# Moving the second half's query loads to another place in the DMA order, and reordering the first three turns of a fused decoder layer

## The chip, the cores and the metric

The kernel runs on one core of a Trainium2 chip. The metric is the device time of one execution in microseconds, the median over several runs.

## The reference

One decoder layer on x (8 batches, 100 tokens, 512 features) with a context of 722 rows per batch. The change touches the middle part, the cross attention:

```python
x = x + rg_lru(layernorm(x))                       # gates, a scan over the tokens, an output product
ln = layernorm(layernorm(x), gamma_lat, beta_lat)  # latents, the queries' source
xn = layernorm(ctx, gamma_media, beta_media)       # 722 rows per batch
q = ln @ Wq + bq
k, v = split(concatenate([xn, ln]) @ Wkv + bkv)
out = softmax(q * DH**-0.5 @ k.T) @ v              # 8 heads of 128
x = x + out @ Wo + bo
x = x + moe(layernorm(x))                          # 8 experts, one chosen per token, gelu
```

## The kernel before, in words

The key weights are folded into the queries, so that scores are products of a query row of 512 numbers per head with the normed context itself, and the value weights are applied after the weighted sum over the context. Every float32 product is made of three float32r products: both operands are split into a high part (a copy on ScalarE, `..._h`) and a low part (the difference, on VectorE, `..._l`); `split_products` (L585, L586, L587) issues the three matmuls.

The attention runs in 16 **turns** u = 2b + g: batch b, half g of the heads (4 heads, 100 tokens, 400 columns). The context's 722 rows and the 100 latents make 7 row tiles (KC = 7). Turn u on TensorE is: `scores(u, 0..6)` (six tiles of 12 matmuls, one of 8), with `spread_sums(u-1)` (L1162, small matmuls that sum the weights of the turn before over the partitions) behind tile 3; then the four quarters of `context(u-1)` (20 matmuls each; L585 to L587, L1186, L1187), with `turn_maxima(u)` (transposes, L1149) behind the first quarter and `spread_maxima(u)` (L1156) behind the second. Turn 0 has scores alone.

VectorE in turn u: `weights(u-1)` (sums and low parts of the exponentials, L1961 to L1972; its last sum releases `spread_sums`), `first_maximum` (L1918), `inverse(u-1)` (L1992, waits for `spread_sums`), `last_maximum` (L1924 to L1932, releases `turn_maxima`), `shifts` (L1941 to L1947, writes dg, which `spread_maxima` waits for), `shift` (L1955, the maxima are added to the scores), and `weighted` (L2001, evacuates a quarter of the context). Between these stand the preparations of later turns: `queries(b, g)` (L1735 qt_l<-qf,qt_h), `keys_transposed` (L1893), `keys_centred` (L1882, needs the row means), `rows_stats` (L1719), `rows_norm` (L1731), `rows_low` (L1908). ScalarE has the matching high parts: `queries` (L1446), `evacuate` (L1475), `exponentials` (L1484), `weights_high` (L1490), `rows_high`, `add_shift` (L1498).

Nothing schedules this: each engine has its order written out by hand, and semaphores join them. SyncE issues nearly all DMAs, in one order of its own, and stands at each wait: for batch b of its loop the latents' keys, the raw context rows of b + 2, the half of the queries (b+1, 1), the transposed context `rt` of b + 2, the store of the sum z(b, 0), the queries (b+2, 0), the store of z(b, 1), a bias row. The queries (800 KB per half batch) go through **one** buffer, `qf`; a load waits until VectorE has made the low part of what was there (`s_qtl`). GpSimd issues the small DMAs: `store_mean` writes the row means to DRAM (L919), `load_mean` brings them back as a row on all partitions (L925), and `spread_inverse` does the same with the inverse sums (L930, L932, L935).

```python
                sp.wait_ge(s_qtl, 2 * (b + 1) + 1)
                load_queries(b + 1, 1)
                sp.wait_ge(s_ktl, keys_done(b + 1))
                if b + 2 < B:
                    load_keys(b + 2)
                write_z(b, 0)
```

After turn 15 comes the `tail` list: value products "V", high and low parts of the units "U", splits of the output weights "O", and so on, interpreted on each engine by its own `finish`. The buffers of the value weights share their place with those of the attention: `rt`, `mrow` and `raw1` lie over `wv_h`.

Of the kernel before, what the change touches and what calls it, by code (L numbers as in the profile page):

```python
# [133 lines left out]
def build(nc, a, out):  # L134
# [59 lines left out]
    raws = [raw, mem.over(wv_h, "raw1", [P, KC, D], skip=ND * MEDIA + -(-MEDIA // 16) * 16)]  # L194
    assert ND * MEDIA + -(-MEDIA // 16) * 16 + KC * D <= 2 * ND * INNER
# [263 lines left out]
    tail = [("V", 0), ("C", 0), ("U", 4), ("V", 1), ("O", 0), ("U", 5), ("V", 2), ("O", 1), ("U", 6), ("V", 3), ("O", 2),  # L459
# [130 lines left out]
    with ctx:  # L590
# [3 lines left out]
        def _(sp):  # L594
# [184 lines left out]
            for b in range(B - 1):  # L779
# [23 lines left out]
            sp.wait_ge(s_xnl, 3 * B)  # L803
            sp.dma_start(wv[:], a["Wv"].rearrange("(c p) n -> p c n", p=P)).then_inc(s_wvd, 16)
# [38 lines left out]
        def _(pool):  # L843
# [146 lines left out]
        def _(pe):  # L990
# [271 lines left out]
            for u in range(1, NU):  # L1262
                for c in range(KC):
# [5 lines left out]
                    elif u > 1 and c == 3:  # L1269
# [92 lines left out]
        def _(act):  # L1362
# [137 lines left out]
            def values_high(k):  # L1500
                act.wait_ge(s_wvd, 16)
                act.copy(wv_h[:, k, :], wv[:, k, :]).then_inc(s_wvh, 1)

            def output_high(k):
                if k == 0:
                    act.wait_ge(s_wod, 16)
# [99 lines left out]
            for u in range(1, NU):  # L1606
# [15 lines left out]
                else:  # L1622
                    weights_high(u - 1, 0)
                    evacuate(u, 0)
                    add_shift(u - 2, ND - 1)
# [9 lines left out]
                    else:  # L1635
                        evacuate(u, 2)
                        queries(b, 1)
                        evacuate(u, 3)
                    for c in range(4, KC):
                        evacuate(u, c)  # L1640
                if g and b + 1 < B:
                    for k in range(ND):
                        keys_transposed(b + 1, k)
                elif not g and b + 1 < B:
                    queries(b + 1, 0)
                add_shift(u - 1, 0)
                if u < NU - 1:
# [4 lines left out]
                    exponentials(u, 2)  # L1652
            for part in range(NP):
# [718 lines left out]
```

## Time and profile before

| | us |
|---|---|
| median of 3 runs | 1032.45 |
| the runs | 1032.45, 1033.51, 1027.98 |
| the profiled execution's own time | 1042.73 |
| its span | 1041.0 |
| TensorE busy | 999.5 (96%) |
| VectorE busy | 821.5 (79%) |
| ScalarE busy | 585.0 (56%) |
| mean granted TensorE clock | 0.985 |

The span is what the trace covers, from the first to the last instruction; the 1.7 us around it belong to the execution's own time. Busy shares are means over very unlike stages. In the rows below a time in brackets is the idle time of that engine just before the row, and behind the arrow stands what ended it.

### The profile page before, as it was taken

Reading aid. Unit: us, or ns where it says so; the run is one execution under the profiler, and the core shown is the slowest. Engines: PE = TensorE matmul, PEld = TensorE weight load, DVE = VectorE, ACT = ScalarE, POOL = GpSimd, SP = SyncE. Lnnn points to the kernel's source line nnn. Section 1 sums busy time; section 2 is a strip of 40 time slices with the busy share of each in tenths; the row PEclk is TensorE's granted clock in tenths of the full one; section 3 lists DMA queues with packets and bytes.
Section 4 is the critical chain, followed back from the end, with each engine's and each line's share of the span. In section 5 each row is a group of like instructions: output and inputs, shape, how many; then the busy total and the mean of one; then the engine's idle time right before and its main releaser. Section 6 shows DMA issues by size and latency. Waiting matters only on the chain.

```text
span 1041.0 us, 14901 instructions
## 1 busy us (share of the span) xinstructions
PE 999.5 (96%) x5274; PEld 919.8 (88%) x5275; DVE 821.5 (79%) x1083; ACT 585.0 (56%) x766; POOL 167.7 (16%) x169
## 2 busy tenths in 40 slices
PE   8999999989999999998999999999999999999995
PEld 6969999879999999998999999998867888888884
DVE  7888456898999989897898977885768947938981
ACT  4426565545546565464554646673645846838861
POOL 3715000111111111111111000000111211211220
PEclk9999999989999999999899999999998999999998
DMA  9433879462654818356184212978358956938960
GB/s 266 135 114 122 302 252 290 122 129 73 177 92 116 161 54 193 75 158 119 55 191 77 88 40 95 312 265 291 120 156 295 356 196 214 347 136 281 362 229 8
DMA packets 107117, 183.88 MB, mean 177 GB/s; under 512 B 27936, under 2 KB 48928, under 8 KB 107058
## 3 DMA queue, kind: packets, MB, share of 16 engines
q1 hardware_dynamic: 102834, 172.64, 54.7%
q0 software_dynamic: 4224, 10.46, 4.2%
q8 instruction: 37, 0.61, 0.2%
q14 instruction: 22, 0.18, 0.1%
HBM read 146.94 MB, written 37.11 MB: 177 GB/s over the span
## 4 chain that ended last, share of the span: by engine, by line
PE 66%; DVE 15%; DMA 9%; issue 4%; ACT 2%; SPq 2%; POOL 0%; DVEq 0%; ACTq 0%; POOLq 0%
PE bank L585 19%; PE bank L586 18%; PE bank L587 18%; DMA qf<-scr_q 6%; DVE str__65 L1719 2%; PE bank L1337 2%; DMA w<-in_WoT 1%; PE bank L1061 1%; DVE pa L1955 1%; DVE xt_l L1893 1%; PE bank L1063 1%; PE bank L1062 1%; DMA zr<-scr_z 1%; DVE hs L1808 1%; PE bank L1156 1%
## 5 line engine op out<-in xcount | busy, mean ns | idle before, releaser
L1735 DVE TENSOR_TENSOR wsl<-stage,wsh 128x2048 fp32r<-128x2048 f32 x63 | 143.7, 2291 | 23.6 <-ACT wsh L1525 18.6
L585 PE MATMUL bank<-ph,xn_h 128*128 128x400 f32 x384 | 140.2, 365 | 0.0
L585 PE MATMUL bank<-qt_h,xt_h 128*128 128x400 f32 x384 | 134.3, 350 | 0.0
L586 PE MATMUL bank<-pl,xn_h 128*128 128x400 f32 x384 | 133.4, 347 | 0.0
L586 PE MATMUL bank<-qt_l,xt_h 128*128 128x400 f32 x384 | 132.7, 346 | 0.0
L587 PE MATMUL bank<-ph,xn_l 128*128 128x400 f32 x384 | 132.7, 345 | 0.0
L587 PE MATMUL bank<-qt_h,xt_l 128*128 128x400 f32 x384 | 132.1, 344 | 0.0
L1525 ACT CAST wsh<-stage 128x2048 fp32r<-128x2048 f32 x63 | 120.5, 1919 | 11.0 <-PE bank L587 8.0
L1475 ACT ACTIVATE pa<-bank,rsr 128x400 f32<-128x400 f32 x96 | 56.4, 591 | 76.0 <-PE bank L587 75.9
L1498 ACT ACTIVATE zf<-zf,gbm 128x400 f32<-128x400 f32 x64 | 39.5, 627 | 105.0 <-DVE zf L2001 105.0
L585 PEld LDWEIGHTS bank<-ph,xn_h 128*128 128x128 f32 x384 | 73.3, 191 | 2.5 <-DVE zf L2001 0.6
L586 PEld LDWEIGHTS bank<-pl,xn_h 128*128 128x128 f32 x384 | 73.3, 191 | 2.3 <-issue 0.3
L587 PEld LDWEIGHTS bank<-ph,xn_l 128*128 128x128 f32 x384 | 73.1, 190 | 0.0
L585 PEld LDWEIGHTS bank<-qt_h,xt_h 128*128 128x128 f32 x384 | 72.8, 190 | 0.2
L586 PEld LDWEIGHTS bank<-qt_l,xt_h 128*128 128x128 f32 x384 | 72.6, 189 | 0.2
L587 PEld LDWEIGHTS bank<-qt_h,xt_l 128*128 128x128 f32 x384 | 72.5, 189 | 0.0
L585 PE MATMUL bank<-wsh,xg_h 128*128 128x512 f32 x160 | 64.8, 405 | 2.4 <-issue 2.4
L585 PE MATMUL bank<-wsh,ht_h 128*128 128x512 f32 x160 | 65.1, 407 | 0.0
L587 PE MATMUL bank<-wsh,xg_l 128*128 128x512 f32 x160 | 63.5, 397 | 0.0
L586 PE MATMUL bank<-wsl,xg_h 128*128 128x512 f32 x160 | 63.4, 397 | 0.0
L587 PE MATMUL bank<-wsh,ht_l 128*128 128x512 f32 x160 | 62.6, 391 | 0.0
L586 PE MATMUL bank<-wsl,ht_h 128*128 128x512 f32 x160 | 62.3, 390 | 0.0
(278 smaller groups left out, 2368.7 us busy)
## 6 DMA issues: line engine op xcount, KB each, us to landing
stage<-in_W SPq DMA_DIRECT2D x63, 1024.0 KB, 6.3
scr_q<-st SPq DMA_DIRECT2D x16, 800.0 KB, 6.7
qf<-scr_q SPq DMA_DIRECT2D x16, 800.0 KB, 7.5
scr_z<-zf SPq DMA_DIRECT2D x16, 800.0 KB, 4.5
zr<-scr_z SPq DMA_DIRECT2D x16, 800.0 KB, 6.2
rt<-in_ctxT SPq DMA_DIRECT2D x7, 1444.0 KB, 21.9
raw<-in_ctx SPq DMA_DIRECT2D x8, 768.0 KB, 5.7
raw<-in_ctx SPq DMA_DIRECT2D x8, 512.0 KB
```

Source lines behind the costliest of these rows:

```text
L585: pe.matmul(dest, lh, rh, start=start and k == 0, stop=False)
L586: pe.matmul(dest, lh, rl, start=False, stop=False)
L587: last = pe.matmul(dest, ll, rh, start=False, stop=stop and k == n - 1)
L1061: pe.matmul(wide, high, xa_h[:, c, tokens_and_shift], start=c == 0, stop=False)
L1062: pe.matmul(out_tokens, high, xa_l[:, c, cols], start=False, stop=False)
L1063: last = pe.matmul(wide, low, xa_h[:, c, tokens_and_shift], start=False, stop=c == ND - 1)
L1337: last = pe.transpose(bank[2 + k % 2][:, c * P:(c + 1) * P], hid[k % 2][:, c * P:(c + 1) * P], ident[:])
L1475: act.activation(pa[k][:, c, :], score_bank(u, c)[:, 0:GR], ACT.Identity, scale=rss[b % 2][:, c:c + 1]).then_inc(s_ev, 1)
L1498: act.activation(at, at, ACT.Identity, bias=gbm[:, 1, dc:dc + 1]).then_inc(s_zbeta, 1)
L1525: act.copy(wsh[q][:], (first_last if made_in_place else stage[q % 4])[:]).then_inc(s_wh, 1)
L1719: ch.add(dve.bn_stats(str_[0:r, c, :], r0[0:r, c, :]))
L1735: return dve.tensor_tensor(dst, src, high.bitcast(F32), ALU.subtract)
```

## The change

Six edits, on all engines.

- **Loads.** SyncE requests the queries (b+1, 1) no longer before `rt` of b + 2 (only for b = 0), but those of (b+2, 1) between the stores of z(b, 0) and z(b, 1); the queries (b+2, 0) go ahead of the store of z(b, 0).
- **Splits of queries.** ScalarE and VectorE make `queries(b+1, 1)` at the end of the odd turn 2b+1, in place of `queries(b, 1)` in the even turn 2b.
- **Turns 1 and 2.** VectorE makes `shifts(1)` ahead of `queries(1, 0)` and the four `keys_transposed`, all four `weighted(0, ...)` behind `shift(1)`, and moves `rows_stats(2)`, `rows_norm(1)` and `queries` in turn 2.
- **Sums.** TensorE makes `spread_sums(1)` behind score tile 6 of turn 2 instead of tile 3.
- **Means.** GpSimd stores the means of batch 2 behind `spread_inverse(1)`, no longer ahead of it.
- **Value weights.** `rt` and `mrow` lie over `wv`, `raw1` over `wv_h`; `wv` is loaded in SyncE's loop, `values_high` and two of four `values_low` go into turn 15, and the first split of the output weights ahead of the last `weighted`.

```diff
+    wv = mem("wv", [P, ND, INNER])
     wv_h = mem("wv_h", [P, ND, INNER], F32R)
-    wv = mem("wv", [P, ND, INNER])
...
-    rt = mem.over(wv_h, "rt", [P, ND, MEDIA])
-    mrow = mem.over(wv_h, "mrow", [P, MEDIA], skip=ND * MEDIA)
+    rt = mem.over(wv, "rt", [P, ND, MEDIA])
+    mrow = mem.over(wv, "mrow", [P, MEDIA], skip=ND * MEDIA)
+    raws = [raw, mem.over(wv_h, "raw1", [P, KC, D], skip=ND * INNER - KC * D)]
...
-    tail = [("V", 0), ("C", 0), ("U", 4), ("V", 1), ("O", 0), ("U", 5), ("V", 2), ("O", 1), ("U", 6), ("V", 3), ("O", 2),
+    tail = [("V", 0), ("C", 0), ("U", 4), ("V", 1), ("O", 1), ("U", 5), ("V", 2), ("O", 2), ("U", 6), ("V", 3),
...
-                sp.wait_ge(s_qtl, 2 * (b + 1) + 1)
-                load_queries(b + 1, 1)
+                if b == 0:
+                    sp.wait_ge(s_qtl, 3)
+                    load_queries(1, 1)
                 sp.wait_ge(s_ktl, keys_done(b + 1))
                 if b + 2 < B:
                     load_keys(b + 2)
+                    sp.wait_ge(s_qtl, 2 * (b + 1) + 2)
+                    load_queries(b + 2, 0)
+                else:
+                    sp.dma_start(wv[:], a["Wv"].rearrange("(c p) n -> p c n", p=P)).then_inc(s_wvd, 16)
                 write_z(b, 0)
                 if b + 2 < B:
-                    sp.wait_ge(s_qtl, 2 * (b + 1) + 2)
-                    load_queries(b + 2, 0)
+                    sp.wait_ge(s_qtl, 2 * (b + 2) + 1)
+                    load_queries(b + 2, 1)
                 write_z(b, 1)
...
-                if b + 2 < B:
+                if 0 < b < B - 2:
                     store_mean(b + 2)
                 spread_inverse(2 * b + 1)
+                if b == 0:
+                    store_mean(2)
...
-                    elif u > 1 and c == 3:
+                    elif u > 1 and c == (KC - 1 if u == 2 else 3):
                         spread_sums(u - 1)
...
+                    shifts(1)
                     queries(1, 0)
+                    for k in range(ND):
+                        keys_transposed(1, k)
+                    for part in range(NP):
+                        shift(1, part)
+                    for dc in range(ND):
+                        weighted(0, dc)
+                    continue
+                if u == 2:
+                    weights(1)
+                    first_maximum(2)
+                    inverse(1)
+                    rows_stats(2, 0)
+                    last_maximum(2)
+                    rows_stats(2, 1)
+                    shifts(2)
+                    weighted(1, 0)
+                    queries(1, 1)
+                    weighted(1, 1)
+                    for part in range(NP):
+                        shift(2, part)
+                    weighted(1, 2)
+                    rows_norm(1, 0)
+                    rows_norm(1, 1)
+                    keys_centred(2, 0)
+                    keys_centred(2, 1)
+                    queries(2, 0)
+                    continue
...
-                if g and b + 2 < B:
-                    rows_stats(b + 2, 0)
-                    rows_stats(b + 2, 1)
-                elif not g and b + 1 < B:
+                if g:
+                    if b + 2 < B:
+                        rows_stats(b + 2, 0)
+                        rows_stats(b + 2, 1)
+                    queries(b + 1, 1)
+                elif b + 1 < B:
                     keys_centred(b + 1, 0)
                     keys_centred(b + 1, 1)
             u = NU - 1
             shifts(u)
+            values_low(0)
             weighted(u - 1, 0)
             for part in range(NP):
                 shift(u, part)
             weighted(u - 1, 1)
+            values_low(1)
             first_sum(u)
...
-            for k in range(ND):
+            for k in range(2, ND):
                 values_low(k)
             low_unit(0)
             low_unit(1)
+            output_low(0)
```

What the diff shows less well is what now stands in a row. First VectorE, in turn 1, between the means taken off the keys of batch 1 and the last exponentials' sums (dg is what `spread_maxima(1)` waits for). Before:

```order
L1882 TENSOR_TENSOR rt<-rt,mrow 128x1444 x2
L1735 TENSOR_TENSOR qt_l<-qf,qt_h 128x4x400
L1893 SCALAR_TENSOR_TENSOR xt_l<-rt,gbm,xt_h 128x722 x3
L1941 TENSOR_REDUCE rm<-bank 100x4
L1943 TENSOR_TENSOR rmc<-rm,c_0_106 100x4
L1945 TENSOR_TENSOR nb<-c_0_106,rmc 100x4
L1947 TENSOR_TENSOR dg<-ident,nb 100x400
```

Now:

```order
L1904 TENSOR_TENSOR rt<-rt,mrow 128x1444 x2
L1963 TENSOR_REDUCE rm<-bank 100x4
L1965 TENSOR_TENSOR rmc<-rm,c_0_106 100x4
L1967 TENSOR_TENSOR nb<-c_0_106,rmc 100x4
L1969 TENSOR_TENSOR dg<-ident,nb 100x400
L1757 TENSOR_TENSOR qt_l<-qf,qt_h 128x4x400
L1915 SCALAR_TENSOR_TENSOR xt_l<-rt,gbm,xt_h 128x722 x4
L1977 TENSOR_TENSOR pa_93<-pa_93,bank 128x1200 x2
```

The four instructions that lead to dg moved ahead of one split of queries and four of keys.

Second VectorE, at the border of every later odd turn and the even turn behind it (here turns 7 and 8), from the last row statistics to the first maximum of the even turn. Before:

```order
L1724 BN_AGGR mvr_104<-str__65 82x2
L2001 TENSOR_TENSOR zf_82<-bank,inv 128x4x100
L1961 TENSOR_TENSOR sm<-pa_93 128x800
L1735 TENSOR_TENSOR pl_96<-pa_93,ph_94 128x1200
L1965 TENSOR_TENSOR sm<-sm,pa_93 128x800
L1735 TENSOR_TENSOR pl_96<-pa_93,ph_94 128x1200
L1969 TENSOR_TENSOR sm<-sm 128x400
L1972 TENSOR_TENSOR sm<-sm,pa_93 54x400
L1735 TENSOR_TENSOR pl_96<-pa_93,ph_94 54x400
L1735 TENSOR_TENSOR qt_l<-qf,qt_h 128x4x400
L1918 TENSOR_TENSOR mx<-pa_91 128x800
```

Now:

```order
L1746 BN_AGGR mvr_104<-str__65 82x2
L1757 TENSOR_TENSOR qt_l<-qf,qt_h 128x4x400
L2023 TENSOR_TENSOR zf_82<-bank,inv 128x4x100
L1983 TENSOR_TENSOR sm<-pa_93 128x800
L1757 TENSOR_TENSOR pl_96<-pa_93,ph_94 128x1200
L1987 TENSOR_TENSOR sm<-sm,pa_93 128x800
L1757 TENSOR_TENSOR pl_96<-pa_93,ph_94 128x1200
L1991 TENSOR_TENSOR sm<-sm 128x400
L1994 TENSOR_TENSOR sm<-sm,pa_93 54x400
L1757 TENSOR_TENSOR pl_96<-pa_93,ph_94 54x400
L1940 TENSOR_TENSOR mx<-pa_91 128x800
```

One split of queries moved from behind the sums (L1972, now L1994) to ahead of them.

Third VectorE, the end of turn 2 as it stands now, from the last quarter but one of the context to the first sum of turn 3 (`raw_80` is the buffer of batch 1's rows, `mrow` the means of batch 2):

```order
L2023 TENSOR_TENSOR zf_99<-bank,inv 128x4x100
L1753 SCALAR_TENSOR_TENSOR raw_80<-raw_80,mvr_104,gm 128x512 x5
L1753 SCALAR_TENSOR_TENSOR raw_80<-raw_80,mvr_104,gm 82x512
L1904 TENSOR_TENSOR rt<-rt,mrow 128x1444 x2
L1757 TENSOR_TENSOR qt_l<-qf,qt_h 128x4x400
L2023 TENSOR_TENSOR zf_99<-bank,inv 128x4x100
L1983 TENSOR_TENSOR sm<-pa_91 128x800
```

The norms of batch 1's rows and a split of queries, which stood ahead of dg in turn 2, now stand around the keys' centring and ahead of the sums of turn 3.

## Rows read from the trace of the kernel before

**Rows 1.** The page: busy time of each engine.

```profile
PE 999.5 (96%) x5274; PEld 919.8 (88%) x5275; DVE 821.5 (79%) x1083; ACT 585.0 (56%) x766; POOL 167.7 (16%) x169
```

**Rows 2.** Waits on PE, 300 to 640 us: total, times, longest, in us.

```profile
PE bank L1149 <- DVEq L1712: 6.4, 2, 5.2
PE bank L1156 <- DVE dg L1947: 1.8, 3, 0.7
```

**Rows 3.** Timeline of PE: start us, us, line, operation, count, [idle before <-releaser].

```profile
210.84 1.65 PE L1156 MATMUL bank<-dg,ones 100*128 100x400 f32 x2 [4.25 <-DVE dg L1947]
...
227.55 1.13 PE L1162 MATMUL bank<-ones,sm 128*100 128x1 f32 x8 [1.73 <-DVEq L1712]
...
235.59 0.35 PE L1141 MATMUL bank<-qt_l,xt_h 128*128 128x400 f32 x1
...
239.22 0.35 PE L1187 MATMUL bank<-pl,xn_h 128*128 128x400 f32 x1
...
260.15 0.43 PE L1162 MATMUL bank<-ones,sm 128*100 128x1 f32 x4
...
416.76 0.61 PE L1162 MATMUL bank<-ones,sm 128*100 128x1 f32 x6
...
699.95 0.45 PE L585 MATMUL bank<-z_h,wv_h 128*128 128x400 f32 x1 [1.48 <-DVE z_l L1735]
```

**Rows 4.** Busy time, granted clock and DMA share of single stretches.

```profile
core 0: us, PE busy (x) PEld busy (x) DVE busy (x) ACT busy (x) POOL busy (x), PEclk, DMA share, GB/s
208.00:216.00 8.00, 5.17 (x18) 4.49 (x19) 7.90 (x12) 2.46 (x3) 0.88 (x1) 0.79 0.60 197
228.00:232.00 4.00, 4.00 (x17) 3.97 (x17) 4.00 (x6) 0.00 (x0) 0.58 (x1) 0.57 0.75 53
492.00:504.00 12.00, 8.28 (x32) 7.94 (x33) 8.81 (x14) 2.78 (x3) 4.50 (x5) 0.72 0.19 50
696.00:704.00 8.00, 6.53 (x32) 5.90 (x33) 8.00 (x9) 7.69 (x10) 0.00 (x0) 1.00 0.89 309
391.80:416.40 24.60, 24.60 (x137) 24.25 (x137) 23.54 (x37) 13.68 (x19) 2.85 (x4) 1.00 0.89 204
```

**Rows 5.** Timeline of DVE, turns 1 and 2, and the last sum of turn 7.

```profile
200.91 3.23 DVE L1882 TENSOR_TENSOR rt<-rt,mrow 128x1444 f32<-128x1444 f32 x2 [0.21 <-DVE mx L1932]
204.06 1.82 DVE L1735 TENSOR_TENSOR qt_l<-qf,qt_h 128x1600 fp32r<-128x1600 f32 x1
205.80 2.73 DVE L1893 SCALAR_TENSOR_TENSOR xt_l<-rt,gbm,xt_h 128x722 fp32r<-128x722 f32 x3
...
208.44 0.68 DVE L1941 TENSOR_REDUCE rm<-bank 100x4 f32<-100x512 f32 x1
...
212.55 3.18 DVE L1955 TENSOR_TENSOR pa<-pa,bank 128x1200 f32<-128x1200 f32 x3
...
221.58 0.98 DVE L1961 TENSOR_TENSOR sm<-pa 128x800 f32<-128x800 f32 x1
...
230.80 4.03 DVE L1731 SCALAR_TENSOR_TENSOR raw<-raw,mvr,gm 128x512 f32<-128x512 f32 x6
...
235.13 0.99 DVE L1924 TENSOR_TENSOR mx<-mx,pa 128x800 f32<-128x800 f32 x1 [0.30 <-ACT pa L1475]
...
415.77 0.57 DVE L1972 TENSOR_TENSOR sm<-sm,pa 54x400 f32<-54x400 f32 x1
```

**Rows 6.** Timeline of POOL: an inverse sum on its way through DRAM.

```profile
263.74 0.67 POOL L930 DMA_DIRECT2D scr_inverse<-iv  x1 [19.89 <-DVE iv L1992]
...
269.75 0.98 POOL L935 COPY inv<-sm 128x400 f32<-128x400 f32 x1 [3.35 <-DMA sm<-scr_inverse]
```

**Rows 7.** DMAs that touch mvr (stores of the means).

```profile
DMA to landing us min/median/max: 8.5/10.4/12.8
```

**Rows 8.** DMAs that touch mrow (loads of the means).

```profile
DMA to landing us min/median/max: 3.5/3.7/5.5
```

**Rows 9.** The chain, 455 to 490 us: start us, us, what.

```profile
461.00 23.67 DMA qf<-scr_q
```

**Rows 10.** DMAs that touch qf (loads of queries).

```profile
DMA to landing us min/median/max: 4.8/7.5/23.7
```

More of the change, by code:

```diff
@@ L1624, in _ @@
                     evacuate(u, 0)
-                    add_shift(u - 2, ND - 1)
+                    if u > 2:
+                        add_shift(u - 2, ND - 1)
                     weights_high(u - 1, 1)
@@ L1636, in _ @@
                         evacuate(u, 2)
-                        queries(b, 1)
                         evacuate(u, 3)
+                        if u == 2:
+                            for dc in range(ND):
+                                add_shift(0, dc)
                     for c in range(4, KC):
@@ L1643, in _ @@
                         keys_transposed(b + 1, k)
+                elif u == 2:
+                    queries(1, 1)
                 elif not g and b + 1 < B:
                     queries(b + 1, 0)
+                elif u == NU - 1:
+                    for k in range(ND):
+                        values_high(k)
+                if u == 1:
+                    for part in range(NP):
+                        exponentials(1, part)
+                    continue
                 add_shift(u - 1, 0)
@@ L2130, in _ @@
                         keys_centred(1, half)
+                    shifts(1)
                     queries(1, 0)
-                else:
-                    weighted(u - 2, ND - 1)
-                    weights(u - 1)
-                    if g:
-                        rows_low(b, 0)
-                        first_maximum(u)
-                        inverse(u - 1)
-                        rows_low(b, 1)
-                        rows_low(b, 2)
-                        last_maximum(u)
-                    else:
-                        queries(b, 1)
-                        first_maximum(u)
-                        inverse(u - 1)
-                        rows_norm(b, 0)
-                        rows_norm(b, 1)
-                        last_maximum(u)
+                    for k in range(ND):
+                        keys_transposed(1, k)
+                    for part in range(NP):
+                        shift(1, part)
+                    for dc in range(ND):
+                        weighted(0, dc)
+                    continue
+                if u == 2:
+                    weights(1)
[6 more added lines that the diff above has]
+                    weighted(1, 0)
+                    queries(1, 1)
+                    weighted(1, 1)
+                    for part in range(NP):
+                        shift(2, part)
[4 more added lines that the diff above has]
+                    keys_centred(2, 1)
+                    queries(2, 0)
+                    continue
+                weighted(u - 2, ND - 1)
+                weights(u - 1)
+                if g:
+                    rows_low(b, 0)
+                    first_maximum(u)
+                    inverse(u - 1)
+                    rows_low(b, 1)
+                    rows_low(b, 2)
+                    last_maximum(u)
+                else:
+                    first_maximum(u)
+                    inverse(u - 1)
+                    rows_norm(b, 0)
+                    rows_norm(b, 1)
+                    last_maximum(u)
                 if u == NU - 1:
@@ L2186, in _ @@
             inverse(u)
-            for k in range(ND):
+            for k in range(2, ND):
                 values_low(k)
```

16 lines of the change are left out of this document (9 added, 7 removed).

## The prediction

> **What bounds the kernel now.** First the page: TensorE is busy 999.5 of 1041.0 us, VectorE 821.5 [rows 1]. So a change that adds no matmul can win only TensorE's idle time, 41 us over the whole program, and the time that its matmuls take too long after its clock has fallen. Second, who makes TensorE wait, in its list of waits and its timeline. In turns 1 and 2 it waits 4.25 us for dg (`shifts(1)`) and 1.73 us for the sums of turn 1 [rows 3]. From 300 to 640 us it waits five times, 8.2 us together, of which one is 5.2 us (turn 9, at the maxima) and four others, with 0.7 the longest of their three at dg, make 3.0 us [rows 2]. Third, the clock in the windows around them: behind the 4.25 us it is 0.79 over 8 us, a loss of 0.21 x 8 = 1.7 us; behind the 1.73 us 0.57 over 4 us, again 1.7 us; around the 5.2 us 0.72 over 12 us, 3.4 us at most, and I take 2.6 us since part of it fell into the wait. These are stretches at the lower of the two levels, 1.2 instead of 2.4 GHz. Behind a wait of 1.48 us at 700 us it stayed at 1.00 [rows 3, 4]. Fourth, what lies behind the 5.2 us: the chain shows a load of queries of 23.67 us, against a median of 7.5 [rows 9, 10]; VectorE stood behind it, in front of the even turn's maxima.
>
> Fifth, VectorE itself. In turns 1 and 2 it has almost no idle time: it is VectorE, not TensorE, that sets the pace there. And in the later odd turns it is just as tight: from 391.8 to 416.4 us it is busy 23.54 of 24.6 us, the rest being the small spaces between dependent instructions [rows 4]; its last sum of turn 7 ends at 415.77 + 0.57 = 416.34 and TensorE needs it at 416.76 [rows 3, 5]. That is a margin of 0.42 us, 0.3 after the 0.1 that a released instruction takes.
>
> **Turns 1 and 2: +2.9 us.** Durations are distances between starts in rows 5: centring 3.15, a split of queries 1.74, a split of keys 0.88, the four instructions to dg 2.3 (208.44 to the 210.78 just before TensorE's release), `shift` 3.1, a `weighted` 0.5, the sums 5.9 (to 227.44) and 0.6 for the last low part, the norms 4.0, `last_maximum` 2.7, a `first_maximum` 0.9. The two `rows_stats` take 2.5 each (what lies between `shift` and the sums less one `weighted`). A matmul takes 3.63/20 = 0.18 [rows 3].
>
> Now VectorE goes: centring to 204.05, dg at 206.4, queries 208.1, four keys 211.6, `shift` 214.7, four `weighted` 216.7, weights 223.2, first maximum 224.1. TensorE, free for dg at 206.6, no longer waits 4.25 us; it makes one quarter of context and starts the scores of turn 2 at 211.7, when the keys are there. But `spread_sums(1)` now stands behind all 80 matmuls of them: 211.7 + 14.5 = 226.2, done at 226.8. VectorE has to wait for it in `inverse(1)`, 2.7 us, where it waited for nothing before. Then statistics 229.3, last maximum 232.0: TensorE, through a quarter at 230.5, waits 1.5 us for it. Statistics, dg at 236.8, then one `weighted`, queries, `weighted`, `shift`, `weighted`, norms: 247.1.
>
> There stands the centring of batch 2's keys, and it needs the row of means. GpSimd now stores the means behind `spread_inverse(1)`: released at 226.9, 7.0 us for the way of the inverse through DRAM (263.74 to 270.73) [rows 6], so 233.9; the second of two stores starts 0.9 us later and lands after 10.4 (8.5 to 12.8) [rows 7], at 245.2; the load takes 3.7 (3.5 to 5.5) [rows 8]: 249.0. VectorE waits 1.9 us. Then 3.15 + 1.74 + 0.5 + 5.9 = 11.3: the sum of turn 2 at 260.3, and TensorE can make its `spread_sums(2)` at 260.4, where it made it at 260.15 [rows 3]. Its own work would have brought it there at about 253.6 (dg at 236.8, 0.8 for its two small matmuls, two quarters 7.3, four score tiles of 12 matmuls 8.7), so it waits some 7 us in one piece, longer than the 5.2 us, and the clock falls behind it: 2.6 us as there. Together 0.3 + 2.6 = +2.9. The gain of 4.25 and 1.73 us at TensorE is not there to be had, because VectorE's same work, with two new waits, decides.
> Bounds: with the means in time and a clock loss of 1.7 only, -0.1; if dg's four instructions also take 0.7 less each time, -1.5. With 12.8 and 5.5 for store and load, the wait is 6.1 us and the clock costs 3.4: +8.3.
>
> Here the Trainium skill says something else (DMA: Bandwidth & Descriptors, "Anatomy of one DMA", the gpsimd path): a DMA takes about 2.0 us and its bytes over 436 GB/s, by which a store of 1.5 KB would be an estimated 2.0 us and the means never late. The rows have 8.5 to 12.8 [rows 7], so the trace does not agree, and the sum goes by the rows.
>
> **Turns 4 to 14: +7.2 us, and -4.2 us.** The split of queries (b+1, 1), 1.74 us, moves from behind the last sum to ahead of the chain that leads to it, and nothing leaves that chain: from the evacuations that TensorE releases to the sum it holds the same instructions as before. So at each `spread_sums` of an odd turn TensorE will wait 1.74 - 0.3 = 1.43 us. Turns 6, 8, 10 and 12 have this margin (0.41 or 0.42), turn 4 even less; turn 14 has 1.6 and is left out. 5 x 1.43 = 7.2. Bounds: 5.0 (if half of the small spaces close up) and 8.7 (1.74 each).
> In exchange the four small waits of the even turns go, -3.0 [rows 2], and an ordinary one of 1.2 in the place of the long one, together -4.2: they come from the split of queries and the late landing ahead of the maxima; now one split stands there, loaded earlier, and TensorE is later by 1.4. For the long one see below. Nothing else in the even turn changes: the queries (b+2, 0) are requested some 7 us earlier, and those of (b+2, 1) a whole turn before use, so a landing of 23.67 us [rows 9] is hidden there. Behind SyncE's new wait stands the store of z(b, 1) alone, whose data come half a turn later anyway; z(b, 0) is needed only a turn on.
>
> **Value weights and tail: -0.5 us.** `values_low(1)` stands ahead of the first sum of turn 15 and delays it by some 0.8 us; a split of the output weights leaves the tail's chain ahead of the wait of 1.48 us [rows 3] and shortens it by up to 1.2. Bounds -1.5 and +0.8. The weights' load, 2 MB, moves to a stretch with little other traffic: nothing.
>
> **The sum.** Against the profiled execution: 1042.73 + 2.9 + 7.2 - 3.0 - 7.8 (5.2 and 2.6 of clock) - 0.5 = 1041.5. That execution is 10.3 us above the median of the runs, and the long wait of 7.8 us explains most of it, so I take it that the median run does not have it, only an ordinary wait of 1.2 us in its place. Against the median then: 1032.45 + 2.9 + 7.2 - 4.2 - 0.5 = **1037.9 us**. With the bounds of the terms it is 1031 to 1045.
>
> **The rivals.**
> - *The long wait was in the median run too.* For it: one load of sixteen took 23.67 and the runs spread over 5.5 us. Against it: the 10.3 us. Then 1032.45 + 2.9 + 7.2 - 3.0 - 7.8 - 0.5 = 1031.3.
> - *Faster: VectorE has room.* The waits at the sums and the early stall do not appear, because what I read as a full VectorE gives way once queries never hold it, and the loads' waits were everywhere: 1032.45 - 3.0 - 7.8 - 0.5 = 1021.2; with half of the new waits 1026. For it: VectorE is busy only 79% overall [rows 1]. Against: rows 4 and the margin of 0.42.
> - *Slower: waits of 1.4 us bring the clock down.* It fell behind 1.73 us but not behind 1.48 [rows 3, 4]. If it falls five times for 1.7 us: 1037.9 + 8.5 = 1046.4. It decides as soon as the waits reach the 1.7 us of turn 2.
> - *The first half's queries become the late ones, so the change only moves the wait.* They are now requested behind `rt` and beside the stores of the means, and needed 0.5 + 6.5 + 1.0 + 4.0 + 2.7 = 14.7 us later, less 1.5 for the high part. 7.5 us [rows 10] is in time; 23.67 each time would cost (23.7 - 13.2 - 2 of margin) + 2.6 per batch, 11 us, and even two such batches give 1060. The Trainium skill speaks for this rival (same page, "Issuing engines are not separate DMA queues"): DMAs of all engines interleave on the same 16 engines. What the row shows is that a load of queries beside such traffic took three times the median.
> - *The means come as that page prices them.* No wait at the centring, sum of turn 2 at 258.5 instead of 260.3: 1037.9 - 1.8 = 1036.1. The landings speak against it [rows 7].
>
> **How the numbers follow.** The forecast has 0.43, half of it above 1037.6 and half within 0.5% (a measurement of this kernel can tell about 0.5%, 5 us, from no change); the long wait in the median 0.15 (same); room on VectorE 0.20 (faster); the clock 0.10 (slower); late first halves 0.06 (slower); means in time 0.06 (same). Faster 0.20, same 0.42, slower 0.38. The range from 1026 to 1046 leaves out most of the rival with room and the worst of the slow ones.
>
> **What would show it.** TensorE's wait for dg in turn 1 is gone; a new one of some 7 us before `spread_sums(2)`, followed by a granted clock near 0.7; VectorE waits for GpSimd's DMA ahead of the centring of batch 2 (about 2 us) and for TensorE in `inverse(1)` (about 3 us). `spread_sums` of turns 5, 7, 9, 11 waits 1.4 us each at a clock of 1.00; the maxima and dg of even turns wait for nothing, and no load of queries appears in the chain. If TensorE waits at the sums of odd turns less than 0.5 us, or reaches the end of turn 2 before 255 us, the prediction is wrong.

## The result, and the profile after

| | before | after |
|---|---|---|
| median, us | 1031.14 | 1049.49 |
| runs, us | 1027.98 to 1033.51 (4) | 1048.25 to 1052.54 (4) |
| ratio, 95% interval | | 1.0184 [1.0147, 1.0222] |
| profiled execution, us | 1042.73 | 1049.27 |
| span, us | 1041.0 | 1047.5 |
| mean granted clock | 0.985 | 0.978 |

The change makes the kernel 1.8% slower: 18.35 us between the medians. The forecast of 1037.9 us had added 5.4 us to the median it started from (1032.45), and 1049.49 lies above its range. Later, in the series of the experiments, the changed kernel had a ratio of 1.014 [1.0071, 1.0210] to the kernel before beside it. The profiled execution of before is 11.6 us above its own median; a second profile of it (first experiment, "the good profile" from here on) has no such long wait, and is the better one to subtract.

Busy time of the engines, which answers to [rows 1]: 4.2 us more on TensorE for the same matmuls, at a mean granted clock of 0.978 in place of 0.985.

```profile
PE 1003.7 (96%) x5274; PEld 923.4 (88%) x5275; DVE 818.9 (78%) x1083; ACT 585.0 (56%) x766; POOL 171.8 (16%) x169
```

Waits on TensorE from 300 to 640 us (total, times, longest), the answer to [rows 2]. All waits at the maxima and at dg are gone; one kind is left, at the sums of the odd turns (turn 3's, at 298 us, lies just outside the stretch).

```profile
PE bank L1167 <- DVEq L1734: 5.0, 4, 1.3
```

TensorE's timeline (start, duration, line, operation, count, [idle time before and what ended it]), the answer to [rows 3]. L1154 are the maxima, L1167 the sums.

```profile
232.70 0.64 PE L1154 MATMUL bank<-ident,mx 128*100 128x128 f32 x4 [1.74 <-DVEq L1734]
...
263.19 1.49 PE L1167 MATMUL bank<-ones,sm 128*100 128x1 f32 x8 [9.19 <-DVEq L1734]
...
298.03 0.87 PE L1167 MATMUL bank<-ones,sm 128*100 128x1 f32 x8 [1.53 <-DVEq L1734]
...
361.55 0.87 PE L1167 MATMUL bank<-ones,sm 128*100 128x1 f32 x8 [1.25 <-DVEq L1734]
...
426.51 0.87 PE L1167 MATMUL bank<-ones,sm 128*100 128x1 f32 x8 [1.26 <-DVEq L1734]
...
706.58 0.45 PE L585 MATMUL bank<-z_h,wv_h 128*128 128x400 f32 x1 [0.35 <-DVE z_l L1757]
```

The waits of 4.25 and 1.73 us in turns 1 and 2 have gone. In their place stand 1.74 us at the maxima of turn 2 and 9.19 us at its sums. Turn 3 waits 1.53 us at its sums, turns 5, 7, 9 and 11 wait 1.25 to 1.27 each. The wait before the value product fell from 1.48 to 0.35 us.

Granted clock in single stretches (columns as in [rows 4]):

```profile
core 0: us, PE busy (x) PEld busy (x) DVE busy (x) ACT busy (x) POOL busy (x), PEclk, DMA share, GB/s
258.00:262.00 4.00, 0.00 (x0) 0.00 (x0) 3.93 (x5) 3.96 (x7) 0.00 (x0) 0.50 0.94 325
262.00:266.00 4.00, 2.81 (x12) 2.80 (x13) 3.82 (x7) 4.00 (x8) 0.00 (x0) 0.50 0.29 71
298.00:302.00 4.00, 3.97 (x26) 3.97 (x27) 3.93 (x7) 0.60 (x1) 0.58 (x1) 1.00 0.60 86
426.00:430.00 4.00, 3.49 (x18) 3.46 (x19) 3.85 (x8) 0.00 (x0) 0.58 (x1) 0.75 0.57 56
430.00:434.00 4.00, 4.00 (x20) 3.98 (x20) 2.06 (x4) 1.16 (x2) 0.00 (x0) 0.82 0.75 310
```

Behind the 9.19 us, at 263, TensorE is at the lower level (0.50); behind the 1.53 us at 298 it stays at 1.00; behind the 1.26 us at 426 it has lost (0.25 + 0.18) x 4 = 1.7 us. Behind the sums of turns 5, 9 and 11 the same 1.7 us are lost. Behind the 1.74 us at the maxima of turn 2 the clock stayed at 1.00.

VectorE and GpSimd in turn 2, the answers to [rows 5] and [rows 6]:

```profile
227.28 0.18 DVE L2014 RECIPROCAL iv<-bank 100x4 f32<-100x4 f32 x1 [3.37 <-PE bank L1167]
...
251.85 1.66 DVE L1904 TENSOR_TENSOR rt<-rt,mrow 128x1444 f32<-128x1444 f32 x1 [4.60 <-DMA mrow<-scr_rows]
```

```profile
234.09 0.78 POOL L922 DMA_DIRECT2D scr_rows<-mvr  x1
...
235.41 0.77 POOL L922 DMA_DIRECT2D scr_rows<-mvr  x1 [0.55 <-DVEq L1734]
...
244.84 0.55 POOL L928 DMA_DIRECT2D mrow<-scr_rows  x1 [8.66 <-DMA scr_rows<-mvr]
```

VectorE waits 3.37 us for the sums behind tile 6 and 4.60 us for the row of means. GpSimd stores the means only when the inverse has come back (234.09), both stores have landed at 244.8, and the load takes another 7.0 us until VectorE goes on.

### The profile page after: what moved, and what is told of

Read it like the earlier page. It is cut to its first block, busy times and chain, and to the rows that moved or that the text cites. A ratio compares the mean times of both kernels' runs of the same rounds, so it can differ in the third digit from the quotient of the medians.

```text
span 1047.5 us, 14907 instructions
## 1 busy us (share of the span) xinstructions
PE 1003.7 (96%) x5274; PEld 923.4 (88%) x5275; DVE 818.9 (78%) x1083; ACT 585.0 (56%) x766; POOL 171.8 (16%) x169
## 4 chain that ended last, share of the span: by engine, by line
PE 76%; DVE 12%; issue 5%; DMA 3%; ACT 2%; POOL 0%; SPq 0%; DVEq 0%; ACTq 0%; POOLq 0%
PE bank L585 21%; PE bank L586 20%; PE bank L587 20%; DVE str__65 L1741 2%; PE bank L1342 2%; DVE xt_l L1915 2%; DVE pa L1977 1%; PE bank L1167 1%; PE bank L1066 1%; PE bank L1068 1%; PE bank L1067 1%; DVE zf L2023 1%; DMA xin<-in_x 1%; PE bank L1146 1%; PE bank L1145 1%
## 5 line engine op out<-in xcount | busy, mean ns | idle before, releaser
L585 PE MATMUL bank<-qt_h,xt_h 128*128 128x400 f32 x384 | 137.0, 357 | 0.3 <-issue 0.3
L586 PE MATMUL bank<-qt_l,xt_h 128*128 128x400 f32 x384 | 135.3, 352 | 0.0
L587 PE MATMUL bank<-qt_h,xt_l 128*128 128x400 f32 x384 | 134.7, 351 | 0.0
L1532 ACT CAST wsh<-stage 128x2048 fp32r<-128x2048 f32 x63 | 120.5, 1919 | 14.5 <-DMA stage<-in_W 8.8
L586 PE MATMUL bank<-wsl,ht_h 128*128 128x512 f32 x160 | 62.3, 390 | 0.0
```

The source lines that it names most:

```text
L585: pe.matmul(dest, lh, rh, start=start and k == 0, stop=False)
L586: pe.matmul(dest, lh, rl, start=False, stop=False)
L587: last = pe.matmul(dest, ll, rh, start=False, stop=stop and k == n - 1)
L1532: act.copy(wsh[q][:], (first_last if made_in_place else stage[q % 4])[:]).then_inc(s_wh, 1)
```

## The experiments

They ran in four groups on four chips, each beside the kernel before on the same chip, where its median was 1036 to 1039 us: the first five rows of the table but "changed, again" on one; "tile 4, no means stored", both "splits back" and "first turns alone" on the next; the other two without the means' stores, "value weights alone" and "statistics first" on the third; "changed, again" and "means first" on the last. So the ratio to the kernel before is what can be compared across them, and its intervals are wide (0.3 to 0.7% to each side). Beside it stand marks, each from one profile: *first turns* is the distance between the starts of the inverses of turns 0 and 3 on VectorE, *a batch* a quarter of that between turns 3 and 11, *way* the time from the inverse of an odd turn (5, 7, 9, 11; it is made in the even turn behind) to the start of its copy on all partitions by GpSimd. The first profile of the changed kernel has 101.2, 64.6 and 10.3 to 10.9, so its two profiles differ by 1.7 us in the first turns and by 0.1 us in a batch.

| kernel | ratio [95%] | first turns | a batch | way |
|---|---|---|---|---|
| before, again | 1.0000 [0.9959, 1.0041] | 96.4 | 62.9 | 8.5 to 10.3 |
| changed, again | 1.0140 [1.0071, 1.0210] | 102.9 | 64.7 | 11.2 to 11.9 |
| sums behind tile 4 | 1.0172 [1.0113, 1.0232] | 102.2 | 65.5 | 12.3 to 13.3 |
| filled waits | 1.0148 [1.0087, 1.0209] | 103.3 | 65.0 | 13.0 to 13.8 |
| first turns old | 1.0109 [1.0049, 1.0169] | 99.8 | 65.0 | 11.8 to 12.3 |
| tile 4, no means stored | 0.9991 [0.9959, 1.0023] | 103.4 | 62.1 | 6.3 to 7.6 |
| changed, no means stored | 1.0122 [1.0071, 1.0173] | 103.2 | 65.0 | 6.1 to 6.4 |
| filled, no means stored | 1.0093 [1.0056, 1.0130] | 104.0 | 63.9 | 6.1 to 6.5 |
| splits back | 0.9974 [0.9943, 1.0005] | 100.7 | 62.2 | 9.5 to 10.4 |
| splits back, first turns old | 0.9935 [0.9894, 0.9976] | 96.8 | 62.7 | 9.8 to 11.0 |
| first turns alone | 1.0024 [0.9988, 1.0060] | 100.6 | 63.9 | 9.0 to 10.9 |
| value weights alone | 0.9989 [0.9951, 1.0028] | 96.7 | 64.7 | 8.0 to 10.5 |
| statistics first | 0.9993 [0.9964, 1.0022] | 102.2 | 62.3 | 9.0 to 11.0 |
| means first | 1.0007 [0.9973, 1.0041] | 103.0 | 62.3 | 9.4 to 10.8 |

### Both kernels once more

> The kernel before, once more, for a second profile of it. Theory 'the long wait is a disturbance': no load of queries near 23.67 us, no wait of 5.2 us in turn 9, and a span near 1030 us instead of 1041. Rival 'it belongs to the kernel': a wait of 4 to 6 us at the maxima of some even turn again, span 1035 to 1041. Time against the kernel before: ratio 1.000, and its interval says how fine the comparison is.

Span 1033.2 us, no wait of 5.2 us, the longest load of queries in the attention 19.7 us. But its ten runs went from 1034.8 to 1044.0, so neither theory holds in full: by their times, some executions have a long wait and some not. The waits on TensorE from 300 to 640 us in this good profile, 2.1 us in all:

```profile
PE bank L1149 <- DVEq L1712: 1.5, 2, 0.9
PE bank L1156 <- DVE dg L1947: 0.6, 1, 0.6
```

> The changed kernel once more, beside the kernel before, on the chip of the experiments: its first result came from another one. Expected ratio 1.013 to 1.020, four batches of 65.0 us, waits of 1.26 us at the sums of turns 5 to 11. If it is under 1.010, what is said of the splits' place is too large.

As expected, with two exceptions. The first of the four batches (65.3 us) had a further wait of 1.5 us for an evacuated quarter in turn 4, and the second took 63.4 us in place of 65.0. There the wait at the sums (1.25 us, at 364.31) was as long as elsewhere, and the clock stayed up:

```profile
core 0: us, PE busy (x) PEld busy (x) DVE busy (x) ACT busy (x) POOL busy (x), PEclk, DMA share, GB/s
364.00:368.00 4.00, 3.69 (x24) 3.69 (x25) 3.85 (x8) 0.48 (x1) 0.58 (x1) 1.00 0.68 50
```

### The sums of odd turns one tile later

```diff
-                    elif u > 1 and c == (KC - 1 if u == 2 else 3):
+                    elif u > 1 and c == (KC - 1 if u == 2 else 4 if 4 <= u < NU and u % 2 == 0 else 3):
```

> The changed kernel with the sums of odd turns 3 to 11 made behind score tile 4 instead of 3, that is one tile of 12 matmuls (2.2 us) later on TensorE; nothing else moves. Theory 'the waits at the odd sums and the clock behind them': five waits (1.53 and four of 1.26) and four falls of the clock (1.7 us each) go, 6.6 + 6.8 = 13.4 us, 1049.5 - 13.4 = about 1036 us. Rival 'waits alone, the clock falls for another reason': 1043 us. Rival 'VectorE sets the pace of the odd turns anyway': the wait comes back at the next place that needs VectorE, and the time stays within 2 us of 1049.5.

(The edit moves the sums of turn 13 as well.) The waits at the sums were gone, and nothing was won: 1.0172. TensorE (first row) now waited for the evacuated quarter, VectorE (second) for the inverse sums, and GpSimd's timeline shows why: 7.7 us from the inverse's store to the load that waits for it, 5.1 more to the copy.

```profile
446.26 0.45 PE L585 MATMUL bank<-ph,xn_h 128*128 128x400 f32 x1 [2.79 <-DVE zf L2023]
```

```profile
445.63 1.06 DVE L2023 TENSOR_TENSOR zf<-bank,inv 128x400 f32<-128x400 f32 x2 [3.97 <-POOL inv L938]
```

```profile
421.80 0.75 POOL L922 DMA_DIRECT2D scr_rows<-mvr  x1 [1.69 <-DVEq L1734]
...
431.85 0.58 POOL L933 DMA_DIRECT2D scr_inverse<-iv  x1 [9.30 <-DVE iv L2014]
...
439.52 0.58 POOL L935 DMA_DIRECT2D sm<-scr_inverse  x1 [7.08 <-DMA scr_inverse<-iv]
...
444.66 0.89 POOL L938 COPY inv<-sm 128x400 f32<-128x400 f32 x1 [4.56 <-DMA sm<-scr_inverse]
```

The third theory is the nearest, but what sets the pace is not VectorE's work: it idles 4 us. It is the way of the inverse through DRAM, which begins with the sums.

### The waits filled with matmuls

```diff
+                pe.wait_ge(s_dg, u + 1)
+                if u % 2 and 3 < u < NU - 1:
+                    keep_running(mbank, xn_h[:, 0, :], 6)
                 pe.wait_ge(s_sum, u + 1)
-                pe.wait_ge(s_dg, u + 1)
```

> The changed kernel with six matmuls whose result nobody reads (512 columns each, some 1.3 us) ahead of TensorE's wait for the sums of turns 5, 7, 9, 11 and 13: TensorE is no longer idle there, but nothing comes earlier. Theory 'half of what the waits cost is the clock behind them': the granted clock stays at 1.00 behind the sums, and the time falls by 4 x 1.7 = 6.8 us to about 1042.7 (turn 13 pays some 1.1 us of filler for nothing: about 1044). Rival 'the clock falls at those places whatever TensorE does in the wait': 1049.5 to 1051 and the windows behind the sums stay at 0.75 to 0.8.

The clock behind the sums stayed at 1.00, where the changed kernel has 0.75 and 0.82:

```profile
core 0: us, PE busy (x) PEld busy (x) DVE busy (x) ACT busy (x) POOL busy (x), PEclk, DMA share, GB/s
426.00:430.00 4.00, 4.00 (x23) 3.91 (x22) 3.96 (x4) 3.13 (x6) 0.00 (x0) 1.00 0.55 24
430.00:434.00 4.00, 4.00 (x26) 3.60 (x26) 3.82 (x8) 0.16 (x2) 0.59 (x1) 1.00 0.89 37
```

The same held at the three other filled waits, and at turn 3's, left unfilled, the clock fell behind 1.63 us. So the fall belongs to TensorE's idling. But the time did not follow (1.0148), for the reason of the run before: no longer slowed by the clock, TensorE now reached the third quarter too early, and waited 0.8 to 1.7 us there for the first to be evacuated.

### The inverse's way without the stores of the means

> The kernel with the sums behind tile 4, and besides, for the batches from 3 on, the row means are not stored (one row in place of 128; the row of batch 1's means is loaded instead, so the outputs are not the layer's). What it is for: with the sums behind tile 4 the waits at the sums went, but TensorE then waited 1.8 to 3.2 us once a batch for the first evacuated quarter, since VectorE waited 4 us for the inverse sums, whose way through DRAM took 13.1 us (store 7.6, load 5.0) in even turns. Theory 'that store lies behind the element-wise stores of the means on the DMA engines': without them the store takes about 2 us as in the last even turn, the way 6 to 8 us, no wait for the quarter, a batch takes 62.6 us as before instead of 64.7, and the time is about 4 x 2.1 to 5 x 2.1 = 8 to 10 us under that of the sums behind tile 4, or 5 to 7 us above the kernel before. Rival 'it is the loads of queries and keys': the way stays above 11 us and a batch at 64.7.

```diff
-                    pool.dma_start(d_row[b].rearrange("(c p) -> p c", p=P)[:, cs], mvs[b % 2][:, cs, 0],
+                    n = P if b < 3 else 1
+                    pool.dma_start(d_row[b].rearrange("(c p) -> p c", p=P)[0:n, cs], mvs[b % 2][0:n, cs, 0],
...
-                pool.dma_start(mrow[:], bc(d_row[b, 0:MEDIA], MEDIA)).then_inc(s_mrow, 16)
+                pool.dma_start(mrow[:], bc(d_row[b if b < 3 else 1, 0:MEDIA], MEDIA)).then_inc(s_mrow, 16)
```

(Against the changed kernel the sums also stand behind tile 4 here.) The way fell from about 13 to between 6.3 and 7.6 us, a batch from 65.5 to 62.1, the ratio from 1.0172 to 0.9991. Of 300 to 640 us only one wait of TensorE was left:

```profile
PE bank L1155 <- DVEq L1735: 0.3, 1, 0.3
```

The stores of the means are what makes the inverse late. They also stretch the loads of the first halves' queries, which are requested just behind them: 4.9 to 5.2 us without the stores, 12.1 to 12.8 with them, at the same place behind the keys.

> The changed kernel as it is, but for the batches from 3 on the row means are not stored (one row in place of 128; batch 1's row is loaded, so the outputs are not the layer's). Theory 'the stores of the means cost time only through the inverse's way, and in the changed kernel the waits at the sums come first': the way shortens to 6 to 8 us, but the waits of 1.26 us at the sums and the clock falls behind them stay, a batch takes 64.5 to 65 us, ratio to before about 1.015 to 1.018. Rival 'the traffic of the means slows the changed kernel by itself': ratio near 1.005.

The way 6.1 to 6.4, the waits at the sums as in the changed kernel (below, with turn 3's now inside the stretch), a batch 65.0. In the changed kernel the sums bind first, and the way second, close behind.

```profile
PE bank L1168 <- DVEq L1735: 6.6, 5, 1.5
```

> The changed kernel without the stores of the means from batch 3 on (as above) and with six matmuls of 512 columns that nobody reads ahead of the waits for the sums of turns 5 to 13: the sums come when they came, but TensorE is busy meanwhile. Without the means' stores the inverse is in time, so the waits for the first quarter do not come. Theory 'half of the cost is the clock': it stays at 1.00 behind the sums and a batch takes 1.7 us less than in the kernel without filler, 63.2 us; 4 x 1.7 = 6.8 us less in all, ratio about 1.010. Rival 'the clock costs nothing, something else is just as late': no difference to the kernel without filler beyond 1 us.

The last three batches took 63.4 to 63.5 us each in place of 65.0, and the span fell from 1051.9 to 1047.0; the first, with turn 3's unfilled wait and a fall behind it, took 65.1. So the clock alone is 1.5 to 1.6 us a batch. The intervals of the two ratios overlap, so this rests on the profiles, on the single batch of 63.4 us above, and on the first batch of the changed kernel's first profile, which took 63.5 us where the clock stayed up behind turn 3's wait.

### The splits put back

```diff
+                    queries(b, 1)
                     first_maximum(u)
                     inverse(u - 1)
...
-                    queries(b + 1, 1)
```

(ScalarE's high parts move in the same way, and SyncE asks for z(b, 0), (b+2, 0), (b+2, 1) in this order)

> The changed kernel with the splits of the second half's queries put back behind the sums of the even turn (VectorE and ScalarE); the load (b+2, 1) stays a turn early, directly behind the load (b+2, 0), the store of z(b, 0) goes ahead of both as before; first turns and tail as changed. Theory 'the split ahead of the odd turn's sums is what costs 2.35 us per batch': no waits at the odd sums, the way of the inverse no longer decides (the sums come 1.7 us earlier), a batch takes 62.6 us or less, and the time is 13 to 14 us below the changed kernel: about 4 us above the kernel before (early turns +5.1, tail -1.2). Rival 'the early load's traffic costs it': a batch stays at 64 us or more, 10 us or more above the kernel before.

0.9974, a batch 62.2 us. All that is left of TensorE's waits between 300 and 640 us:

```profile
PE bank L1161 <- DVE dg L1969: 0.4, 1, 0.4
```

The whole loss of the later turns went with this edit, that is with the place of one split of 1.8 us on VectorE, ScalarE's copy for it, and the order of z(b, 0) and (b+2, 0) on SyncE; these three were not tried one by one. The early load of (b+2, 1) is not its cause, since it stayed.

### The first turns

> The changed kernel with its first three turns put back as they were before (VectorE, ScalarE, the sums of turn 1 behind tile 3, the means of batch 2 stored ahead of the second inverse); the loads' new place and the splits at the end of odd turns stay from turn 3 on. Theory (trace marks): the early part costs 5.1 us, so about 1044.4. By the prediction's own price of 2.9: 1046.6. Rival 'early order is neutral, both stalls only swapped': 1049 to 1050.

1.0109 against 1.0140 for the changed kernel (measured on another of the chips). A batch is 65.0 as there; the first turns are 3.1 us shorter than in its second profile, 1.4 than in its first, nearer to the prediction's own price of 2.9 than to 5.1. They still hold a wait of 3.1 us for the inverse in turn 2.

> The kernel before with the reordering of the first three turns alone (VectorE, ScalarE, the sums of turn 1 behind tile 6, the means of batch 2 behind the second inverse). Theory: +5.1 us (wait of 9 us at the sums of turn 2 and its clock, against 4.25 and 1.73 and theirs), ratio 1.005. The prediction's price was +2.9, ratio 1.003. Rival 'it is neutral': 1.000.

1.0024, which the interval [0.9988, 1.0060] does not tell from no change; in the profile the first turns are 4.2 us longer than before, with this wait at the sums of turn 2:

```profile
262.71 1.50 PE L1164 MATMUL bank<-ones,sm 128*100 128x1 f32 x8 [8.44 <-DVEq L1727]
```

> The kernel with the splits put back (first turns as changed), with the first half of the row statistics of batch 2 ahead of the inverse of turn 1 on VectorE in turn 2, where it waits 3.4 us for TensorE's sums. Theory 'the two waits of VectorE in turn 2 make the early loss': 2.5 us of work fill that wait, the means are stored 2.5 us earlier, the wait at the sums of turn 2 falls from 8 to some 5.5 us: 2.5 us less than the kernel with the splits put back, ratio about 0.995. Rival 'the means' way decides by itself': the wait at the sums stays at 8.

The rival holds. VectorE was some 2.5 us earlier, and waited that much longer for the means (6.09 us where it waited 3.58 with the splits put back), whose stores start at 234.74 as ever, behind the inverse. The sums came at 263.3 as there (263.0), and TensorE, earlier too, waited 10.7 us for them in place of 8.1:

```profile
251.97 1.66 DVE L1904 TENSOR_TENSOR rt<-rt,mrow 128x1444 f32<-128x1444 f32 x1 [6.09 <-DMA mrow<-scr_rows]
```

> The kernel with the splits put back (first turns as changed), with both row statistics of batch 2 ahead of the inverse of turn 1 on VectorE, and the means stored ahead of the second inverse on GpSimd, as before the change. Theory 'the early loss is the means' way (stored only after the inverse has been through DRAM)': the means are there when VectorE needs them, its wait of 3.6 us for them goes, the wait at the sums of turn 2 falls from 8.1 to 5 or 6 us, ratio 0.994 to 0.996. Rival 'now the inverse's store stands behind the means' and its way takes 10 us instead of 6': VectorE waits 2 to 3 us for the inverse instead, the sums of turn 2 come at the same time within 1 us, ratio 0.997 to 0.999.

The rival again, and stronger than its text. Now the inverse's store (230.46) stood behind the two of the means, the way took 13.1 us in place of 6, and VectorE waited 8.7 us for it. TensorE's long wait broke in two, 6.9 us for the evacuated quarter and 3.5 at the sums, which came 2.2 us later than with the splits put back:

```profile
243.54 0.57 DVE L2021 TENSOR_TENSOR zf<-bank,inv 128x400 f32<-128x400 f32 x1 [8.72 <-POOL inv L938]
```

```profile
230.46 0.59 POOL L933 DMA_DIRECT2D scr_inverse<-iv  x1
...
239.02 0.58 POOL L935 DMA_DIRECT2D sm<-scr_inverse  x1 [7.98 <-DMA scr_inverse<-iv]
```

So in turn 2 either the means stand behind the inverse or the inverse behind the means. It is not bandwidth here: while the inverse's store was under way the 16 DMA engines were busy for 6% or less and moved 4 GB/s at most.

```profile
core 0: us, PE busy (x) PEld busy (x) DVE busy (x) ACT busy (x) POOL busy (x), PEclk, DMA share, GB/s
228.00:232.00 4.00, 3.65 (x20) 3.32 (x19) 3.63 (x10) 1.27 (x1) 1.36 (x2) 1.00 0.06 1
232.00:236.00 4.00, 3.62 (x22) 3.62 (x23) 1.86 (x5) 0.00 (x0) 0.00 (x0) 1.00 0.06 4
```

### A version that beats both

> The kernel before with the new order of the value weights alone (their buffer, the load in SyncE's loop, splits in turn 15, the first split of the output weights). Theory: the wait of 1.48 us ahead of the value product shrinks to 0.35, ratio 0.999. Then the rest of the 0.9935 of the kernel with early loads and this order belongs to the loads. Rival 'the value weights bring most of it': ratio 0.995.

0.9989. Its profile shows again the late load of turn 9, in the chain and before the maxima:

```profile
461.12 23.02 DMA qf<-scr_q
```

```profile
495.19 1.09 PE L1149 MATMUL bank<-ident,mx 128*100 128x128 f32 x4 [5.52 <-DVEq L1716]
```

> The kernel before with only the load (b+2, 1) requested a turn early and the new order of the value weights: first turns and all splits of queries as before. Theory: the small waits for the queries in even turns (0.5 to 0.95 us each) go, the tail gives 1.2 us: 2 to 4 us below the kernel before, ratio 0.996 to 0.998; a load of 20 us has no effect. Rival 'two loads in a row lie in the way of the inverse sums': ratio 1.002 or more, with a wait for the first quarter.

0.9935 [0.9894, 0.9976], some 5 to 7 us under the kernel before (4.7 between the medians, 0.65% by the ratio). Its ten runs went from 1030.0 to 1037.0; the ten with the value weights alone from 1030.3 to 1045.1. Of the small waits it kept four, 2.9 us at dg, so that part of its theory is wrong:

```profile
PE bank L1159 <- DVE dg L1954: 2.9, 4, 1.2
```

So the gain is most likely the long wait, which by their times none of its ten runs had. Only one of them has a profile, whose span, 1032.7 us, is 0.5 under the good profile's. The times point the same way: of the 79 runs of the kernel before beside the experiments 23 lie above 1041 us, of the 50 runs of the five kernels with the early load and a batch of 62 to 63 us only one does, by 0.3 us. What the early load is worth apart from the value weights is not told by the two ratios (0.9935 and 0.9989), whose intervals overlap.

## Why the prediction was wrong, point by point

The waits were foreseen, and nearly in size. What failed is the step that kept the clock at 1.00 behind the waits at the sums of the odd turns: it put at nothing what measured 6.8 us. The rest of the miss is spread over smaller terms and a part that stays open.

- **Early stall gone, new wait in turn 2** (predicted 7 us, here 9.19; 2.7 and 1.9 for VectorE, here 3.37 and 4.60). Right in kind and place. The term of +2.9 measured 4.2 us in the marks (first turns alone; splits back against the same with old first turns, 100.7 - 96.8 = 3.9). In the changed kernel itself it is 101.2 - 96.4 - 1.5 = 3.3, and 5.0 in its second profile (the 1.5 is turn 3's wait, counted below). Mis-sized was the load of the means, 7.0 us where [rows 8] gave 3.7 with 5.5 at most.
- **Odd turns: 5 x 1.43 = +7.2.** Right in kind, place and size: 1.53 + 1.25 + 1.26 + 1.27 + 1.26 = 6.6 us, turn 14 free.
- **"at a clock of 1.00": the step that failed.** The forecast kept the clock up, since it had fallen behind 1.73 but not behind 1.48 us, and gave the rival of a falling clock 0.10. It fell behind four of the five waits, and a term that stood at nothing came to 4 x 1.7 = 6.8 us; filling the waits took 1.5 to 1.6 of them away in each batch. The rival's threshold ("it decides as soon as the waits reach the 1.7 us of turn 2") was wrong as well: it fell behind 1.25 and not behind 1.74. Two rows do not make a threshold in length. This alone does not carry the forecast out of its range: 1037.9 + 6.8 = 1044.7.
- **Even turns -4.2.** Measured as some -3.4: from the inverse of turn 3 to that of turn 11 the changed kernel has 5.0 us of new waits and three falls of the clock, 5.1 us, together 10.1, but this stretch grew only from 251.7 (the good profile) to 258.4 us, 6.7. The waits that went are 2.1 us of it there; for the other 1.3 no row was found. The waits themselves went as said (no maxima or dg in the list), and no load of queries stood in the chain.
- **Tail -0.5.** -1.1 at the wait before the value product. It does not show in the whole stretch from the inverse of turn 13 to the end: 424.3 to 425.3 us in the profiles with the old order of the value weights, 423.4 to 426.8 with the new one.
- **The sum.** 4.2 + 6.6 + 6.8 - 3.4 - 1.1 = 13.1 us. The good profile and that of the changed kernel differ by 1047.5 - 1033.2 = 14.3, the later ratio of 1.0140 makes 14.5, the first comparison 18.4. Of the last, 3.8 us are that the good profile, 1034.9 us in all and taken later, lies above the first median of before; why the kernel before ran faster then is open. Of the 14.3, some 1.2 us are missing in the sum, and the marks show that the terms do not fit everywhere: up to the inverse of turn 3 the profiles differ by 4.3 us (terms: 4.2 + 1.5), to that of turn 11 by 6.7 (by how the -3.4 was got), and behind it by 3.4 (terms: 1.7 of clock - 1.1), so 2.8 us of the end have no term. With the measured sizes the forecast's own sum is 1032.45 + 13.1 = 1045.6; the rest up to 1049.5 is not explained by it.
- **The rivals.** "The long wait was in the median run too" seems to hold for some executions (3 of the 10 runs of the first experiment lie above 1041 us), not for the median. "VectorE has room" fell: nothing closed up. "The first half's queries become late" fell: their loads did grow, from 4.8 to 7.8 us before to 11.3 to 11.9 from batch 3 on, but stayed within the 13.2 us that the rival itself allowed, and nothing waited for them. What no rival had is the inverse's way through DRAM: in turn 8 its copy ended at 439.5 (438.61 + 0.90) and VectorE used it at 441.0, so at most 1.5 us of any gain at the sums was to be had.
- "The means come as that page prices them" (1036.1) fell: the landings of the means' stores stayed at 8.4 to 11.3 us against the 2.0 that the Trainium skill's rule gives (DMA: Bandwidth & Descriptors, "Anatomy of one DMA"). By the same rule the inverse's store of 1.6 KB would be late nowhere; here it took 2.0 us alone and 8.6 behind the stores of the means.

## What to carry to other kernels

Price a new wait of a full TensorE twice, once for its length and once for the clock behind it, unless rows of waits like it, many of them, show that the clock stays up. Before moving work ahead of a chain whose margin is 0.4 us, ask what is next in line: here the inverse's way stood 1.5 us behind the sums, and removing the waits at the sums alone gave nothing. And a load's request and the work that uses it can be moved apart: the early request did no harm and most likely took the long wait away, the moved split cost what the change lost in the later turns.

## What the hardware showed

- Waits of equal length at one place of the program brought the clock down or not: 1.25 us at 361.55 did and, in another execution, 1.25 us at 364.31 did not; 1.53 us at the sums of turn 3 did not, while 1.54 and 1.55 us there did in two of the other kernels (no means stored; first turns old). With the sums behind tile 4, waits of 2.4 to 2.8 us for an evacuated quarter in turns 8, 10 and 12 left it at 1.00, and one of 1.8 us in turn 6 did not. What decides is open.
- A small store behind other small stores is slow: the inverse's 1.6 KB took 2.0 us where no stores of the means were under way (227.76 to 229.75) and 8.6 us behind two of them (230.46 to 239.02), with the DMA engines 6% busy. That the stores of the means delay it is shown by leaving them out; by what was not tried, but in turn 2 it was not a lack of bandwidth.
- A load's length depends on what is under way beside it. In the old place, ahead of the keys, the loads of the second half's queries took 13.5 to 19.5 us from batch 2 on (second profile of before), 23.0 in one with the value weights alone. In the changed kernel those of the second halves, in their new place, took 4.2 to 4.5 us from batch 3 on (4.2 to 6.3 in its second profile) and those of the first halves, now right behind the keys and beside the stores of the means, 11.3 to 11.9 (12.1 to 12.7). Without those stores the first halves' took 4.8 to 5.4 at the same place, so the stores of 1.5 KB stretch them, directly or by way of the keys' load, which itself took 10.8 to 12.7 us without them and 11.1 to 17.6 with them. The stores of z(b, 0), 800 KB, took 5.7 to 6.8 us without them and 13.3 to 15.0 with them. Whether the same holds in the old place was not tried.
